# New slots for every step, and identity products on TensorE, in a four-layer transformer kernel

## What is computed

```
x = x + attn_a(layernorm(x))     # latent attention, 16 heads, causal softmax
x = x + ffn(layernorm(x))        # token shift, sigmoid(r) * (relu(k)**2 @ W_v)
x = x + attn_b(layernorm(x))     # 16 heads of 8, q and k normalised, scale 8, causal softmax
x = x + ffn(layernorm(x))

ffn(x):    xr, xk = mu_r*x + (1-mu_r)*x_prev, mu_k*x + (1-mu_k)*x_prev   # x_prev: the token before
           return sigmoid(xr @ W_r) * (relu(xk @ W_k)**2 @ W_v)
attn_b(x): q, k = l2norm(x @ Wq), l2norm(x @ Wk); v = x @ Wv             # per head
           return softmax(mask(8 * q @ k.T)) @ v @ Wo
```

## Time and profile before

| | |
|---|---|
| median of 3 runs | 1086.67 us (1085.28 to 1087.6) |
| the profiled execution's own time | 1086.84 us |
| its span, first to last instruction | 1085.1 us |
| mean granted clock of TensorE in it | 0.946 |
| busy: TensorE, weight loads, VectorE | 948.4, 519.7, 876.0 us |
| busy: ScalarE, GpSimd | 768.9, 282.1 us |
| DMA | 112.95 MB, mean 104 GB/s |

### The profile page before, as it was taken

One profiled execution on the slowest core, in us unless ns is written; L12 is line 12 of the kernel. 1 busy time (PEld: TensorE's weight loads), 2 busy tenths in 40 slices (PEclk: granted clock), 3 DMA queues, 4 the chain that ended last, 5 costly groups with the idle time before them and its releaser, 6 DMA issues.

```text
span 1085.1 us, 37311 instructions
## 1 busy us (share of the span) xinstructions
PE 948.4 (87%) x15889; PEld 519.7 (48%) x15889; DVE 876.0 (81%) x2112; ACT 768.9 (71%) x1042; POOL 282.1 (26%) x264
## 2 busy tenths in 40 slices
PE   3688889799889899999989899999989899898794
PEld 1334445354455455454545455454545545454352
DVE  3978978888788898989898988889888987764633
ACT  2165677577757778887878777787868777788681
POOL 6111213123122232223223232323222231223212
PEclk8599989899989999999999999999999999899897
DMA  5244433346327162633627180624527180504130
GB/s 146 71 105 101 119 95 80 89 114 176 82 73 184 35 173 53 165 94 104 154 69 188 36 211 19 189 64 120 139 82 176 36 211 3 129 3 127 60 70 19
DMA packets 94342, 112.95 MB, mean 104 GB/s; under 512 B 15200, under 2 KB 81888, under 8 KB 94176
## 3 DMA queue, kind: packets, MB, share of 16 engines
q1 hardware_dynamic: 94176, 110.56, 39.3%
HBM read 55.22 MB, written 54.53 MB: 101 GB/s over the span
## 4 chain that ended last, share of the span: by engine, by line
PE 58%; DVE 23%; ACT 12%; issue 4%; POOL 2%; DMA 1%; SPq 0%; POOLq 0%; DVEq 0%; ACTq 0%
PE acc L729 20%; PE pool L712 10%; DVE rowmax L1081 9%; ACT prob L930 7%; PE pool L595 5%; PE pool L643 5%; PE pool L762 3%; PE pool L609 3%; PE pool L770 3%; PE pool L659 3%; PE pool L784 2%; ACT vals_a L916 2%; DVE xn L1039 2%; PE pool L802 1%; ACT vals_b L916 1%
## 5 line engine op out<-in xcount | busy, mean ns | idle before, releaser
L930 ACT ACTIVATE prob<-pool 128x1024 f32<-128x1024 f32 x576 | 568.1, 1031 | 137.1 <-PE pool L659 133.4
L1081 DVE TENSOR_REDUCE rowmax<-pool 128x2 f32<-128x1024 f32 (+7 forms) x480 | 357.3, 790 | 59.8 <-PE pool L659 57.2
L729 PE MATMUL acc<-prob,vals_b 128*32 128x512 f32 (+7 forms) x2048 | 170.3, 431 | 1.9 <-issue 0.8
L729 PE MATMUL acc<-prob,vals_a 128*32 128x64 f32 (+7 forms) x2048 | 168.8, 420 | 0.2 <-ACT prob L930 0.2
L643 PE MATMUL pool<-stack_ka,stack_qa 48*64 48x512 bf16 (+7 forms) x2048 | 121.0, 304 | 47.8 <-ACT vals_a L916 15.9
L712 PE MATMUL pool<-stack_qa,stack_ka 51*64 51x512 bf16 (+7 forms) x2048 | 110.5, 296 | 24.0 <-DVE rowmax L1081 12.2
L659 PE MATMUL pool<-mask_t,ident_b 64*64 64x128 bf16 (+1 forms) x2304 | 130.1, 216 | 0.0
L712 PE MATMUL pool<-stack_qb,stack_kb 48*64 48x512 bf16 (+7 forms) x2048 | 114.2, 302 | 9.0 <-DVE rowmax L1081 4.8
L1292 POOL TENSOR_TENSOR rstd<-mv,minus_half 128x4 f32<-128x4 f32 x64 | 65.1, 1018 | 154.5 <-DVE mv L1034 154.5
L643 PEld LDWEIGHTS pool<-stack_ka,stack_qa 48*64 48x64 bf16 x2048 | 43.2, 108 | 128.5 <-issue 65.7
L1304 POOL TENSOR_TENSOR parts_q<-rest_q,parts_q 128x512 bf16<-128x512 f32 x32 | 37.5, 1171 | 176.6 <-DVE parts_q L1055 176.4
(11 more groups left out here) (129 smaller groups left out, 1386.9 us busy)
## 6 DMA issues: line engine op xcount, KB each, us to landing
stack_qa<-scratch_qa SPq DMA_DIRECT2D x64, 192.0 KB, 4.1
stack_ka<-scratch_ka SPq DMA_DIRECT2D x64, 192.0 KB, 4.4
stack_kb<-scratch_kb SPq DMA_DIRECT2D x64, 192.0 KB, 4.4
stack_qb<-scratch_qb SPq DMA_DIRECT2D x64, 192.0 KB, 5.3
scratch_qa<-parts_q SPq DMA_DIRECT2D x16, 384.0 KB, 6.0
scratch_ka<-parts_k SPq DMA_DIRECT2D x16, 384.0 KB, 4.4
scratch_qb<-parts_q SPq DMA_DIRECT2D x16, 384.0 KB, 2.5
scratch_kb<-parts_k SPq DMA_DIRECT2D x16, 384.0 KB, 2.8
```

What stands on the lines that cost most here:

```text
L729: last = eng.matmul(acc[32 * j:32 * j + 32, BLK * blk:T], vals[a][:, blk, GROUP * g + j, :], prob[n % NPROB][:, k, at:at + T - BLK * blk], ...
L930: eng.activation(prob[n % NPROB][:, :, :], place["unit", n][0][:, :, :], ACT.Exp, scale=scale).then_inc(S["exped"], 1)
L1081: last = eng.tensor_reduce(to, of, axis=AX.X, op=ALU.max)
```

## The change

Two things. First, all numbers of `PLANS` are new, in each of its six entries. Second, every TensorE step gets, between the wait for its bank and the wait for its input, a call of `warm`, which multiplies the f32 identity by itself so many times into the first 128 columns of that bank; the step's own first product then overwrites them (`start=True`). How often is a list per entry of `PLANS`, one number for each kind of step, in the order of `WARM_AT`. The list is all zeros for the default entry, so that batches 3 to 13 have none. "ya" and "qk" are reached twice in a batch. The diff, cut: the default entry whole, of the others only the new lists; of the calls of `warm`, four of the thirteen.

```
@@ -26,6 +26,8 @@
 
 STACK = [(0, (0, 0, 0), (0, 1, 2)), (3, (1, 1), (0, 1)), (5, (2,), (0,))]
 
+WARM_AT = ("max", "max rows", "unit", "xnT1", "qa", "ka", "valsa", "ya", "xnT2", "k2", "r2", "v2", "xnT3", "qk", "qb", "kb",
+           "valsb", "wo", "xnT4", "k4", "r4", "v4")
 SLOTS = 36
 LEAD = 3
 
@@ -33,106 +35,112 @@
 
 PLANS = {
     None: {
-        "load": [-124.6],
-        "prepare_front": [-117, -106.5, -100.2, -95, -90.3],
-        "restack_a": [-102.4, -88.1],
-        "row_maxima0": [-64, -60, -55, -51, -47.7, -46, -44.2, -35.5, -35.2],
-        "max_rows0": [-31.5, -22.5],
-        "row_maxima1": [-33, -32.5, -25.5, -20, -15.7, -14.2, -9.2, -7, -6],
-        "max_rows1": [0.5, 2.5],
-        "values_a": [-34.8, -34.5],
-        "half_norm": [30],
-        "middle_front": [37, 39.7, 45, 47.5, 57.5, 57.8, 62, 65, 68.5, 71],
-        "restack_b": [90.6, 103.6],
-        "middle_back": [73, 80, 85, 90, 90, 93, 94, 98, 105, 109, 113],
-        "values_b": [-35.2, -34.6],
+        "warm": [0, 0, 0, 0, 0, 0, 0, 0, 0, 0, 0, 0, 0, 0, 0, 0, 0, 0, 0, 0, 0, 0],
+        "load": [-146.7],
+        "prepare_front": [-118, -106.5, -100.7, -95, -90.3],
+        "restack_a": [-93, -57.1],
+        "row_maxima0": [-64, -60, -55, -51, -48.2, -45, -43.2, -35.5, -35.2],
+        "max_rows0": [-26.7, -22.6],
+        "row_maxima1": [-33.3, -32.5, -25.8, -20.5, -15.7, -13.7, -9.2, -6, -6],
+        "max_rows1": [-1.7, 2.2],
+        "values_a": [-35.3, -35.2],
+        "half_norm": [29.9],
+        "middle_front": [37, 38.7, 45, 48, 57.5, 58.5, 62.3, 65, 70, 70.8],
+        "restack_b": [81.3, 92.5],
+        "middle_back": [74, 80, 85, 90, 90, 92.5, 94, 98, 106, 110, 113],
+        "values_b": [-34.6, -34.5],
         "half_norm_b": [22.4],
-        "finish": [33.5, 35.2, 38.2, 40.2, 44.2, 48.7, 53.2, 54, 57, 57, 62.7, 77.2],
+        "finish": [34.5, 35.2, 38.2, 40.5, 44.2, 48.7, 53.2, 53.7, 57, 57, 63.2, 71.5],
...
     0: {
...
+        "warm": [0, 0, 0, 0, 1, 0, 1, 0, 1, 0, 0, 0, 0, 0, 3, 1, 1, 5, 1, 0, 0, 1],
...
     1: {
...
+        "warm": [0, 0, 0, 6, 0, 0, 0, 5, 0, 0, 0, 0, 2, 0, 0, 1, 1, 0, 6, 6, 0, 0],
...
     2: {
...
+        "warm": [0, 0, 0, 0, 0, 0, 0, 0, 4, 2, 0, 0, 1, 0, 0, 0, 0, 6, 0, 0, 0, 2],
...
     -2: {
...
+        "warm": [0, 0, 0, 0, 0, 0, 0, 1, 3, 0, 0, 0, 0, 0, 2, 2, 0, 0, 0, 0, 0, 0],
...
     -1: {
...
+        "warm": [0, 0, 0, 0, 0, 0, 0, 0, 1, 0, 0, 0, 4, 0, 5, 1, 0, 0, 10, 10, 1, 0],
...
@@ -589,6 +597,12 @@
                     q.wait_ge(S["made"], part[-1] + 1)
                     yield
 
+            def warm(self, ps, at, b):
+
+                plan = PLANS.get(b, PLANS.get(b - B, PLANS[None]))
+                for _ in range(plan["warm"][WARM_AT.index(at)]):
+                    self.eng.matmul(ps[:, 0:P], ident[:, :], ident[:, :], start=True, stop=True)
+
             def product(self, to, lhs, rhs):
 
...
                 yield
                 ps, freed = place["xnT" + n, b]
                 q.wait_free(freed)
+                self.warm(ps, "xnT" + n, b)
                 q.wait_ge(S["xn" + n], b + 1)
...
                     n = len(MAX_UNITS) * (2 * b + g) + i
                     ps, freed = place["max", n]
                     q.wait_free(freed)
+                    self.warm(ps[:, 0, :], "max", b)
                     pieces = sum(max_pieces(*unit, NB), [])
...
                 yield
                 ps, freed = place["k" + n, b]
                 q.wait_free(freed)
+                self.warm(ps, "k" + n, b)
                 q.wait_ge(S["xk" + n], b + 1)
...
                 yield
                 ps, freed = place["wo", b]
                 q.wait_free(freed)
+                self.warm(ps, "wo", b)
                 q.wait_ge(S["yT"], b + 1)
...
```

More of the change, by code:

```diff
@@ L35 @@
     None: {
[L36 to L45, removed]
@@ L51 @@
     },
     0: {
[L53 to L62, removed]
@@ L86 @@
-    2: {
[L87 to L101, removed]
+        "warm": [0, 0, 0, 0, 1, 0, 1, 0, 1, 0, 0, 0, 0, 0, 3, 1, 1, 5, 1, 0, 0, 1],
@@ new lines @@
+        "load": [-135],
+        "prepare_front": [-112.5, -107.8, -106, -106, -100.3],
+        "restack_a": [-51.1, -48],
+        "row_maxima0": [-71.4, -58.5, -49.5, -46.8, -44.9, -40.9, -38.9, -38.2, -38],
+        "max_rows0": [-23.8, -18.5],
+        "row_maxima1": [-34.2, -32, -19.7, -16.5, -15.5, -9.9, -9.5, -7.5, -7.5],
+        "max_rows1": [-2, 6],
+        "values_a": [-28.6, -24.8],
+        "half_norm": [23.8],
+        "middle_front": [33, 36, 38, 43, 47, 52.7, 53, 55, 58, 64.2],
@@ new lines @@
+    2: {
+        "warm": [0, 0, 0, 0, 0, 0, 0, 0, 4, 2, 0, 0, 1, 0, 0, 0, 0, 6, 0, 0, 0, 2],
+        "load": [-100],
+        "prepare_front": [-66.5, -57.5, -55, -53, -49.8],
+        "restack_a": [-69.7, -66.7],
+        "row_maxima0": [-31.2, -26.5, -24.2, -23.2, -20.3, -20, -20, -17, -16.5],
+        "max_rows0": [-11.5, -8.5],
+        "row_maxima1": [-15.5, -14, -13, -12.3, -12, -9.5, -9, -4.2, -2.5],
+        "max_rows1": [7.3, 7.5],
+        "values_a": [-65.7, -36.8],
+        "half_norm": [29.7],
+        "middle_front": [33.5, 35, 39.3, 43.3, 50.3, 55.3, 57.5, 65, 69, 72],
+        "restack_b": [97.6, 123.5],
+        "middle_back": [72, 79, 85.3, 90, 90, 91, 94, 97, 106.6, 110.3, 112.3],
+        "values_b": [-42, -37.2],
+        "half_norm_b": [29.3],
+        "finish": [33, 34.5, 37, 39, 43, 47, 52.3, 53, 54, 56.3, 59.3, 72.3],
@@ L102 @@
     },
     -2: {
[L104 to L118, removed]
+        "warm": [0, 0, 0, 0, 0, 0, 0, 1, 3, 0, 0, 0, 0, 0, 2, 2, 0, 0, 0, 0, 0, 0],
+        "load": [-127.7],
+        "prepare_front": [-116, -107.5, -105, -102.5, -89.8],
+        "restack_a": [-94.2, -93.9],
+        "row_maxima0": [-59.7, -57.7, -56.5, -51, -51, -47.5, -44.5, -37.5, -36],
@@ L119 @@
     },
     -1: {
[L121 to L128, removed]
-        "half_norm": [23.7],
-        "middle_front": [44, 44, 46, 46.5, 56.4, 60.4, 61.7, 63.4, 69.7, 69.7],
```

105 lines of the change are left out of this document (77 added, 28 removed).

## The result

The changed kernel takes 1039.87 us (median of 4 runs, 1036.63 to 1042.75); the kernel before took 1085.97 beside it. The ratio is 0.9561 [0.9535, 0.9587]: 46 us faster, four times the 11.5 I had summed, and outside my range. The profiled execution, the slowest of the four, took 1042.75 us with a span of 1041.0.

A forecast was written before the change was run, and what follows sets the result against it. It took VectorE and TensorE, both near full, to bound the steady middle, with VectorE binding at the turn. Filling -4.0, end -3.0 and middle -4.5 made -11.5 us from 1086.84: 1075, range 1062 to 1094.

The forecast's parts named there:

- The turn: From half a to half b in the steady middle: values_a and q reordered, 0.5 us a period, nine periods, -4.5 us.
- The middle's low clock: Five low stretches, 20.5 us, in the steady middle: no products there, one more or fewer 1.6 us, range only.
- Rival B: The waits were the path: middle gains 1.65 us nine times, filling 7.7, giving 1062.7 us; chance 0.13.
- VectorE's sum is unchanged; nothing: Steady middle: max_rows0 some 5 slots later, max_rows1 ahead of norm1 and yT; priced at nothing.
- I take half: Filling, 54 to 330 us: products remove half the low clock's 15.3 us, -7.7; net -4.0 after their own time.
- the sign that I had named: Low stretches between 54 and 330 us summing to about 17 us, half of 34.1, would show the forecast right.
- The sum for the products, -7: Identity products in filling and end together: -4.0 us in the filling, -3.0 in last halves and tail.
- The tail: Chain after the last weighing: products hold the clock for transposes, k and v; -1.5 us, ends -2.2 and +2.2.
- The last halves: Batches -2 and -1 ahead of the tail: products cut two low stretches; -1.5 us, ends 0 and -7.7.
- Move (b): Steady middle: score unit st3u1 of group 1 goes ahead of row maxima 0.5; nothing, at most one reduction's slack.
- SP and the loads: DMA queue: restack_a 31 slots later, load 22 sooner, store ahead of q's and k's writes; all nothing.
- The start: First 54 us: TensorE waits for VectorE, six products go into a wait; nothing, 1.5 us either way.

The follow-up runs named there:

- e9: Kernel before, no products, with only the turn's three slots new in the default entry (values_a ahead, q one slot later): 1073.37 us.
- e6: Changed kernel with values_a behind norm1 again in the default entry, so the wait for vals_a returns: 1051.40 us.
- e7: Changed kernel with sum1 one slot earlier in the default entry, so GpSimd runs x_a ahead of parts_q: 1043.70 us.
- e10: Changed kernel with the whole turn (values_a and q) as before in the default entry: 1059.23 us, median of three runs.
- e13: Kernel before with the five other entries new, of the default entry only the turn and max_rows0, max_rows1 new, no products: 1047.22 us.
- e4: Changed kernel with the old default entry; the five other entries and their products stay new: 1078.61 us.
- e14: Kernel before with the five other entries' slots new, default entry old, no products: 1075.68 us.
- e8: Changed kernel with max_rows0 and max_rows1 at their old slots in the default entry: 1046.87 us.
- e2: Kernel before with the new lists of identity products in its old slots: 1093.08 us.
- e1: Changed kernel with all lists of identity products set to zero, new slots kept: 1046.89 us.
- e12: Changed kernel with products in the last two batches alone: 1040.37 us.

## Why the prediction was wrong

The direction was right, the size was not: a forecast of 1075, a range from 1062, and 1039.87.

**The turn, the step that failed first.** I wrote that "rest_q ends near 501.3", so that row maxima 1.1 would wait for it, and that of xn's 1.36 us only 0.5 was to be had, since "only x_a is left beside it". On the old scale (offset 24.44) rest_q ended at 500.14 (475.01 + 0.69 + 24.44), row maxima 1.1 ran at 500.37 and the next reductions began at 500.6, not 501.52. The exponential came as I had it: row maxima 1.0 at 499.0 against 498.7. What I missed is that GpSimd has a queue of its own: x_a stands behind parts_q there, and as parts_q now waits for rest_q, both leave xn alone. The move cut TensorE's wait from 1.65 to 0.97 us and took 1.2 us of work a period from VectorE (54.1 to 52.9, e9) at once, which is why "So VectorE binds here" did not hold. With only the wait put back (e6) it is 0.66 us a period, with only the contention (e7) 0.3; with both (e10) 1.7, low clock included.

**The middle's low clock, the second.** I had put it into the range alone, "one more or fewer is 1.6 us either way". All five of the earlier trace rows went, and one of 3.4 us came at 886.2. Low stretches of the kernel before, and what stands ahead of them:

```profile
613.06:619.60 6.54, 4.89 (x72) 2.85 (x67) 6.40 (x12) 4.67 (x8) 2.38 (x2) 0.96 0.37 123
619.60:626.40 6.80, 6.80 (x84) 3.74 (x84) 5.01 (x17) 3.53 (x5) 2.18 (x2) 0.54 0.23 78
674.40:681.00 6.60, 4.40 (x64) 2.99 (x68) 6.46 (x11) 5.46 (x9) 2.38 (x2) 0.96 0.35 119
681.00:684.40 3.40, 3.40 (x36) 1.37 (x32) 2.93 (x6) 0.77 (x1) 0.00 (x0) 0.57 0.02 5
```

TensorE is busy 4.9 of the 6.5 us and 4.4 of the 6.6 ahead of the fall, with the wait of 1.65 us for vals_a in them. Cut finer, all five stretches begin 0.4 to 1.7 us behind the start of row maxima 1.0, which ends that wait (379.6, 439.9, 617.9, 680.1 and 741.3; the stretches at 380.1, 441.6, 619.1, 680.5 and 741.9). Without the wait for vals_a they are gone, in e9, e13 and the changed kernel (which keeps a wait of 0.97 us), with no product anywhere near; with it back (e10) three come back right behind it, at 479.0, 659.9 and 721.3, and two elsewhere. I had priced the wait and the clock as two things and they hang together. Not every such wait brings a low stretch, though: of the six of 1.65 us between b3 and b12 four do in e4, and in e14, the same slots without products, one. Between b3 and b12 the low clock fell from 23.8 us to 3.4, at 0.45 a gain of 9.2 of the 18.3, an estimate. The price looks high: the periods of the kernel before from 764.7 to 887.5 us take 60.9 and 61.9 us at full clock, so not all above 58.89 is clock. Period by period, the four with no low stretch in either kernel are 1.3 us shorter on the mean and the other five 13.1 together, which leaves 6.6 us to the clock, 0.32 for each us, and 11.7 to the rest. Rival B had the wait as the path, but not its price: its 14.9 us (nine times 1.65; the earlier trace rows sums to 14.2) were too little by the low clock behind it.

**The slots in the filling, the third and the largest.** My sum has no term for them: I had read the filling only as 40.5 us of idle TensorE to be covered with products, never by who ends its waits, and gave no price to what the new slots of batches 0, 1 and 2 do there. By b3 they bring 5.1 us (e14, 397.9 against 403.0), and the turn and `max_rows` together another 15.4 (e13). "VectorE's sum is unchanged; nothing" had its premise wrong, as the sum fell by 0.8 us a period (e9 to e13); in the middle "nothing" held all the same (e8), and in the filling the step was the end of a wait of 5.4 us. One view of waits of that stretch would have shown the 6.2 and 3.1 us above. That is the largest miss, 21.4 us against 4.0.

**The products.** "I take half" was right for the clock in e2, 34.1 to 17.0 us, and the net gain was nothing. But half of the low clock goes without any product too: e1 has 17.0 us of it in the filling, so the sign that I had named does not speak for them. The price of 0.45 us for each us of low clock was taken from periods in which TensorE is nearly full; that in the filling it is slow where it would have waited anyway is likely, but no run shows it apart from the products' own time. The rule of the Trainium skill, "TensorE: Matmul & The Clock Gate", Part 1, that I had argued against is about the ramp, whose penalty it puts under 1% of a span; I had stretched it to all low clock. No run here contradicts it: the middle's clock was worth 6.6 to 9.2 us by the sums above, itself under 1%. The sum for the products, -7, lies within what was measured (2 to 7) only because the terms' errors met.

**What held.** The tail: 1.7 us against 1.5. The last halves, b12 to b15, gained 2.7 us against 1.5 (110.7 to 108.0), but that was luck: without any product (e1) they take 108.0 us too, so the slots did it. (The transposes at 1020.80 of the earlier trace rows are batch 15's, not 14's; the five products I gave them are batch 15's.) In the tail the transposes took 0.66, k 1.07 and v 1.16 us:

```profile
1023.46 3.68 PE L604 MATMUL pool<-ident 128*128 128x128 f32 x20
1028.43 0.66 PE L624 MATMUL pool<-ident,xn 128*128 128x128 f32 x4 [1.29 <-DVE xn L1066]
1028.92 2.40 PE L604 MATMUL pool<-ident 128*128 128x128 f32 x20
1031.89 1.07 PE L609 MATMUL pool<-ffn_xk,T_k 128*32 128x512 f32 x8 [0.57 <-DVE ffn_xk L1183]
...
1034.85 1.16 PE L794 MATMUL pool<-T_v,ffn_act 128*128 128x128 f32 x8 [0.58 <-POOL ffn_act L1382]
```

Move (b), SP and the loads at nothing: e13. The start at nothing: half a0 ends at 85.5 us instead of 86.1. The clock there is worth little: e12 runs at half clock for 30.7 us from 19.2 us on, the changed kernel for 20.5, and half a0 ends at 86.3 and 85.5. (e7, e1 and e14 have no clock records for their first 43 to 51 us and read 1.00 there; e7's row maxima at 27 us take 0.64 us a group, as in the changed kernel at half clock, against 0.41 at full clock, so those rows say nothing of the clock.)

## What to carry to other kernels

Where two engines are both nearly full, look at every short wait for what it drags along: here 1.65 us of waiting had a slow clock for 3.4 to 6.8 us behind it in five periods of nine, and the move that shortened it removed a collision of VectorE with GpSimd too. Before pricing a reordering at nothing, list for each stretch who ends its waits, and for each step that gets a new bank, follow the old holder's release back through all the queues it stands in; one step in one slot was worth 31 us. A product that keeps the clock up has to earn its own time too: in the old order 103 of them halved the filling's low clock, and the kernel was no faster.
